# When ScalarE copies the transposed attention, and how many context steps stand ahead of the first norm's transposes in a decoder block

## The chip, the cores and the metric

One core of one Trainium2 chip. The metric is the device time of one launch in microseconds (us); lower is better. A run-time is given as the median of several runs.

## What is computed

A decoder block for 8 batch elements of 512 tokens, width 256, in float32. In words, for each batch element:

- `x = x + attn(layernorm(x))`: self-attention with 16 heads of 16, with learned relative-position terms on scores and values (clipped at a distance of 20), softmax, output projection `Wo`;
- `x = x + xattn(layernorm(x), ctx, ctx)`: a cross-attention without softmax over a context of 1601 rows of width 256, 16 heads of 64. Its inputs pass a layernorm with gain and bias; queries and keys are divided by their L2 norm per head. Behind it an MLP with GELU (width 1024), with residuals of its own;
- `x = x + ffn(layernorm(x))`: a gated feed-forward part (width 704) with blockwise 4-bit quantisation of inputs and weights.

Because the cross-attention has no softmax, `(qn kn^T) v` is computed as `qn (kn^T v)`: the context is folded once per batch element into a matrix per head, and then into one matrix `M` with the output projection.

## The kernel before

**Engines and order.** The kernel is written by engine: each of SyncE, GpSimd, ScalarE, VectorE and TensorE has a hand-written program, a loop over batch elements 0 to 6 (`batch(b, False)`) and a last round for element 7 (`batch(NB - 1, True)`). Each engine works strictly in its own written order; semaphores tie the orders together. The work is cut in T = 4 tiles of 128 tokens.

**The context steps.** While element b is in its tail (all that follows the attention's scores and softmax), the engines fold the context of element b + 1. This is cut in small steps, numbered s = -6 to 25, and each engine has a function `slot(nb, s)` with its share of step s. The 13 context tiles of 128 rows pass twice, each time for half of the heads, so that 26 steps accumulate. What an engine does in step s:

- TensorE (lines 1606 to 1635): two *ck matmuls* (keys of accumulation step s + 3; their moving operand is `cwk`, 512 wide), two *ct transposes* of context tile s + 4 (while there is such a tile), and for s >= 0 four *cg matmuls* which accumulate key-times-context in PSUM banks 4 and 5. At s = 0 and s = 13 the two banks are first zeroed with matmuls of `zeros`, at 13 after the first half has been read out (`evac_g`, L1264 on VectorE, L977 on ScalarE).
- ScalarE (lines 979 to 998): copy of the keys out of PSUM (L985), copy of the transposed context (L990), the squares of the keys (L995).
- VectorE (lines 1266 to 1308): statistics of context tile s + 6 (L1273 to L1278), sums of squares per head for step s + 2 (L1285, L1287), the norm's affine part for tile s + 5 (L1295, L1299), and the scaling of the keys of step s + 1 (L1306). Tiles end at 12, so the statistics end with s = 6 and the affine part with s = 7.
- GpSimd (lines 732 to 739): the inverse roots for both (L429, on `crs` and `crn`).

The waits are such that TensorE's step s needs VectorE's step s - 1 whole: the ct transposes wait for `caff_ready` (L1299), the cg matmuls for `cs_ready` (L1306):

```python
pe.wait_ge(caff_ready, ctile(nb, i))     # i = s + 4, made by VectorE's step s - 1
...
pe.wait_ge(cs_ready, cstep(nb, s))       # made by VectorE's step s - 1
```

VectorE's step s needs ScalarE's squares and GpSimd's roots of step s - 1 (the roots of the statistics too).

**Where the steps stand.** The table `SLOTS_AT` (line 79) puts the steps at named places of the tail, the same on the four engines, and each engine runs `slots(at)` where that place comes in its own order:

- `("band", t)`, steps -6 to -3: behind `weigh_band(t)` on TensorE, `combine(t)` on VectorE, and behind the copy L1136 on ScalarE;
- `("wo", t)`, steps -2 to 1: the output projection of the attention. TensorE (lines 1859 to 1880) transposes `Oraw` of tile t + 1, projects tile t (`project`, which waits for `aT_ready`; the row names `wo_s`), then does the step. ScalarE (lines 1138 to 1144) copies the transposed attention of tile t (L1142, which signals `aT_ready`), then does the step. VectorE (lines 1436 to 1442) adds the projection to `xin` (L1439), takes statistics (L1441), then does the step;
- `"ln"`, steps 2 to 5: TensorE does them directly behind the step of `("wo", 3)`, and only then transposes `Qn` (lines 1883 to 1887). VectorE first does the two chained norms (L1452 to L1467: aggregate, two inverse roots by GpSimd, `Qx`, `Qn`), then the steps, then half of `QnT` (L1471). ScalarE does the steps, then the other half of `QnT` (L1154). GpSimd does the steps between the norm's roots and the query norm's first root;
- `("x", -1)`, steps 6 to 8: behind the query projection of tile 0 (`project_q`, the row names `cwq`) on TensorE, behind the square L1151 on ScalarE, between the sum of squares L1476 of tile 0 and the scaling L1485 of tile 0 on VectorE, behind the query norm's root of tile 0 on GpSimd (L429 on `rn`);
- `("x", t)`, steps 9 to 18: within the cross-attention of tile t, behind the transposes of `qn`. TensorE waits for L1485 of tile t before it projects the queries of tile t + 1;
- `"yn"` and `("h", f)`, steps 19 to 25: norm and MLP.

The last round has no steps: in it `slots` does nothing.

Of the kernel before, what the change touches and what calls it, by code (L numbers as in the profile page):

```python
# [22 lines left out]
T = S // 128  # L23
# [53 lines left out]
LOADS = ((0, 1), (1, 4), (4, 8), (8, 12), (12, 13))  # L77
EQ = HG * 128
SLOTS_AT = {("band", 0): (-6,), ("band", 1): (-5,), ("band", 2): (-4,), ("band", 3): (-3,),
# [3 lines left out]
SLOTS_Q = (0, 0, 0, 1, 1, 1, 2, 2)  # L83
NORM_AT = 5
# [6 lines left out]
def build(nc, bass, mybir, d, out):  # L91
# [5 lines left out]
    with ctx:  # L97
# [147 lines left out]
        def bank(i, lo=0, hi=512, parts=128):  # L245
            return PS[0:parts, i * 512 + lo:i * 512 + hi]
# [726 lines left out]
        def _(act):  # L973
# [5 lines left out]
            def slot(nb, s):  # L979
                j = s + 3  # L980
                if 0 <= j < CSTEPS:
                    n = crows(j % CT)
                    act.wait_ge(ck_psum, cstep(nb, j))
                    act.wait_ge(cg_done, cstep(nb, j - 4))
                    act.activation(kns[0:n, j % 4, :], bank(6, parts=n), ACT.Copy).then_inc(kc_ready, 1)  # L985
                i = s + 4
                if 0 <= i < CT:
                    n = crows(i)
                    act.wait_ge(ct_psum, ctile(nb, i))
                    act.activation(cnT[:, i, :, 0:n], bank(7, 0, 256).rearrange("p (c t) -> p c t", c=2)[:, :, 0:n], ACT.Copy)\  # L990
                        .then_inc(ct_ready, 1)
                if 0 <= j < CSTEPS:
                    act.wait_ge(kc_ready, cstep(nb, j))
                    act.wait_ge(c_norm, cstep(nb, j - 2))
                    act.activation(csq[0:crows(j % CT), j % 2, :], kns[0:crows(j % CT), j % 4, :], ACT.Square)\  # L995
                        .then_inc(csq_ready, 1)
                if s == CT:
                    evac_g(nb, 0)
# [82 lines left out]
            def batch(b, final):  # L1081
                def slots(at):
                    for s in () if final else SLOTS_AT[at]:
                        slot(b + 1, s)
# [47 lines left out]
                for t in range(T):  # L1132
# [2 lines left out]
                        act.wait_ge(f_psum, T * b + t)  # L1135
                    act.activation(AT[:, t % 2, 0:4, :].rearrange("p a b -> p (a b)"), bank(0), ACT.Copy).then_inc(fa_act, 1)  # L1136
                    slots(("band", t))
                for t in range(T):
                    act.wait_ge(at_psum, T * b + t + 2)
                    if t >= 2:  # L1140
                        act.wait_ge(wo_psum, T * b + t)
                    act.activation(aT[:, t % 2, :, :].rearrange("p a b -> p (a b)"), bank(t % 2, 0, 256), ACT.Copy)\  # L1142
                        .then_inc(aT_ready, 1)
                    slots(("wo", t))
                slots("ln")

# [84 lines left out]
            with act.Fori(0, NB - 1) as b:  # L1231
                batch(b, False)
            batch(NB - 1, True)


# [865 lines left out]
```

## Time and profile before

| | |
|---|---|
| median of 3 runs | 2904.91 us (2897.34 to 2914.84) |
| the profiled execution | 2905.99 us, its span 2904.1 us |
| granted TensorE clock, mean | 0.955 |
| TensorE (matmul) busy | 2529.4 us, 87% |
| VectorE / GpSimd / ScalarE busy | 1705.5 / 1437.7 / 1180.0 us |
| chain that ended last | TensorE 64%, VectorE 9%, DMA 8%, issue 8%, ScalarE 6%, GpSimd 3% |

In the profile PE is the TensorE, PEld its weight loads, DVE the VectorE, ACT the ScalarE, POOL the GpSimd, SP the SyncE; L1142 is line 1142 of the kernel. L1601 is the helper through which all matmuls pass and L1604 that of all transposes, so matmuls are told apart by their operands. A float32 matmul shows as two records. In a timeline equal instructions are merged in one row; what follows in brackets is how long the engine was idle before the row and what ended this. A matmul's end overlaps the start of the next. PEclk is the granted TensorE clock as a share of full speed, 2.4 GHz; at 0.5 it is 1.2 GHz.

### The profile page before, as it was taken

The page shows a single profiled execution, that of the slowest core. Times are in us where ns is not written, and L with a number is a line of the kernel's source. Part 1 is how long each engine was busy: PE and PEld are TensorE (multiplying, and loading weights), DVE is VectorE, ACT ScalarE, POOL GpSimd, SP SyncE. Part 2 cuts the span into 40 slices and gives each one's busy share as a digit, 9 for nine tenths or more (in the row PEclk, how much of TensorE's full clock was granted, in tenths as well). Part 3 has the DMA queues.
Part 4 walks back from the last instruction along what each step waited for, and adds up shares of the span by engine and source line. Part 5 has one row for each costly group of instructions (what it writes and reads, how often), then busy time and mean ns, then how long its engine had stood idle before and what let it go on. Part 6 is the DMA issues. An engine that isn't in the chain of part 4 may idle for free.

```text
span 2904.1 us, 49839 instructions
## 1 busy us (share of the span) xinstructions
PE 2529.4 (87%) x14884; PEld 1734.0 (60%) x14884; DVE 1705.5 (59%) x3890; ACT 1180.0 (41%) x2089; POOL 1437.7 (50%) x1489
## 2 busy tenths in 40 slices
PE   3697899888998889988999889988899888998877
PEld 1365566665665656656566655666566565666645
DVE  4746644676446764566646665367654676456625
ACT  1237423382234722355333642338323472235511
POOL 2447444573545645365553745457344564436422
PEclk8799999998999999999999999999999999999989
DMA  8607200670007600284004720057100760028300
GB/s 244 140 0 167 59 1 8 143 181 25 1 27 166 163 1 1 70 160 126 1 8 100 177 71 1 8 132 181 36 1 22 167 167 1 1 68 160 104 0 8
DMA packets 403729, 224.59 MB, mean 77 GB/s; under 512 B 209822, under 2 KB 399542, under 8 KB 400438
## 3 DMA queue, kind: packets, MB, share of 16 engines
q1 hardware_dynamic: 370406, 215.76, 30.6%
q10 hardware_dynamic: 33024, 5.24, 1.6%
q8 instruction: 139, 2.28, 0.3%
q14 instruction: 160, 1.31, 0.2%
HBM read 129.15 MB, written 91.80 MB: 76 GB/s over the span
## 4 chain that ended last, share of the span: by engine, by line
PE 64%; DVE 9%; DMA 8%; issue 8%; ACT 6%; POOL 3%; SPq 1%; ACTq 0%; DVEq 0%; POOLq 0%
PE PS L1601 58%; PE PS L1604 7%; DMA prob_scr<-arena 5%; DMA arena<-bias_scr 2%; ACT arena L1104 1%; ACT arena L1097 1%; DVE PS L1377 1%; DVE ss L1476 1%; DVE arena L1306 1%; POOL rstd L429 1%; SPq L587 1%; ACT arena L1151 1%; POOL arena L769 1%; DVE arena L1295 1%; DVE css L1285 0%
## 5 line engine op out<-in xcount | busy, mean ns | idle before, releaser
L1601 PE MATMUL PS<-arena 128*17 128x128 f32 (+7 forms) x6656 | 746.5, 310 | 84.4 <-ACT arena L1097 66.9
L1601 PEld LDWEIGHTS PS<-arena 128*17 128x17 f32 (+2 forms) x6656 | 498.7, 123 | 272.8 <-issue 125.8
L1604 PE MATMUL PS<-ident,arena 128*128 128x128 f32 (+1 forms) x3312 | 520.3, 285 | 101.1 <-DVE arena L1299 31.1
L1604 PEld LDWEIGHTS PS<-ident,arena 128*128 128x128 f32 (+1 forms) x3312 | 390.4, 145 | 274.0 <-issue 92.4
L429 POOL TENSOR_TENSOR crn<-crn,mhalf 128x8 f32<-128x8 f32 (+1 forms) x208 | 373.5, 1802 | 115.8 <-DVE crn L1287 114.3
L1377 DVE CUSTOM_DVE_ANT_0 PS<-PS,arena 128x512 f32<-128x512 f32 x512 | 343.0, 711 | 125.1 <-POOL arena L769 89.5
L1601 PE MATMUL PS<-cwk,arena 128*128 128x512 f32 (+1 forms) x832 | 406.9, 613 | 2.6 <-ACT arena L990 2.6
L1097 ACT ACTIVATE arena<-PS,nmax 128x512 f32<-128x512 f32 x512 | 344.8, 695 | 113.7 <-DMA prob_scr<-arena 59.5
L985 ACT ACTIVATE arena<-PS 128x512 f32<-128x512 f32 (+1 forms) x208 | 124.2, 597 | 553.7 <-PE PS L1601 553.7
L769 POOL TENSOR_TENSOR arena<-arena 128x128 f32<-128x128 f32 x512 | 218.0, 459 | 102.7 <-DMA arena<-bias_scr 97.4
L1104 ACT ACTIVATE arena<-PS 128x512 f32<-128x512 f32 x384 | 232.5, 606 | 10.5 <-PE PS L1601 9.4
L429 POOL TENSOR_TENSOR rn<-rn,mhalf 128x16 f32<-128x16 f32 x32 | 93.0, 2906 | 286.9 <-DVE rn L1478 286.9
L1601 PEld LDWEIGHTS PS<-cwk,arena 128*128 128x128 f32 (+1 forms) x832 | 158.1, 194 | 126.9 <-issue 114.2
L429 POOL TENSOR_TENSOR crs<-crs,mhalf 128x1 f32<-128x1 f32 (+1 forms) x104 | 64.0, 615 | 271.4 <-DVE crs L1278 271.4
L1285 DVE TENSOR_REDUCE css<-arena 128x8 f32<-128x512 f32 (+1 forms) x208 | 141.7, 681 | 85.8 <-ACT arena L995 85.6
L1306 DVE TENSOR_TENSOR arena<-arena,crn 128x512 f32<-128x512 f32 (+1 forms) x208 | 142.6, 685 | 60.1 <-POOL crn L429 58.0
L870 POOL TENSOR_TENSOR arena<-arena,mass_mask 128x512 f32<-128x512 f32 x128 | 163.7, 1279 | 19.6 <-ACT arena L1097 19.5
L429 POOL TENSOR_TENSOR rstd<-rstd,mhalf 128x4 f32<-128x4 f32 (+1 forms) x48 | 44.7, 931 | 253.8 <-DVE rstd L442 170.3
L757 POOL TENSOR_TENSOR arena<-edge_mask,arena 128x512 f32<-128x512 f32 x128 | 134.4, 1050 | 28.5 <-POOL arena L769 20.3
L1601 PE MATMUL PS<-cwq,arena 128*128 128x512 f32 x256 | 120.6, 615 | 14.2 <-DVE arena L1471 7.2
L995 ACT ACTIVATE arena<-arena 128x512 f32<-128x512 f32 (+1 forms) x208 | 131.1, 630 | 3.6
L1601 PE MATMUL PS<-wdT,arena 128*128 128x256 f32 (+1 forms) x384 | 99.3, 401 | 32.3 <-ACT arena L1194 31.1
(162 smaller groups left out, 3654.9 us busy)
## 6 DMA issues: line engine op xcount, KB each, us to landing
arena<-bias_scr SPq DMA_DIRECT2D x128, 336.0 KB, 3.6
prob_scr<-arena SPq DMA_DIRECT2D x128, 336.0 KB, 4.6
q_scr<-arena SPq DMA_DIRECT2D x128, 128.0 KB
arena<-q_scr SPq DMA_DIRECT2D x128, 128.0 KB, 4.4
arena<-k_scr SPq DMA_DIRECT2D x16, 768.0 KB, 11.9
arena<-prob_scr SPq DMA_DIRECT2D x128, 80.0 KB, 3.4
arena<-far_scr SPq DMA_DIRECT2D x16, 546.0 KB, 7.8
arena<-in_ctx SPq DMA_DIRECT2D x16, 512.0 KB, 5.0
```

Source lines behind the costliest of these rows:

```text
L429: pool.tensor_tensor(x, x, mhalf[0:x.shape[0], 0:x.shape[1]], ALU.pow).then_inc(done, 1)
L757: pool.tensor_tensor(Eb, edge_mask[:].unsqueeze(1).broadcast_to([128, HG, 128]), bcast(Rb[:, t, g * HG:(g + 1) * HG, BAND], 128), ALU.mult ...
L769: pool.tensor_tensor(edge, edge, Eb[:, j, :], ALU.add).then_inc(far_added, 1)
L870: pool.tensor_tensor(prod[:], P[:, (g % 2) * HG:(g % 2 + 1) * HG, t * 128 + BAND:t * 128 + BAND + 128], mass_mask[:].unsqueeze(1).broadcas ...
L995: act.activation(csq[0:crows(j % CT), j % 2, :], kns[0:crows(j % CT), j % 4, :], ACT.Square)\
L1097: act.activation(P[:, (g % 2) * HG + j, PAD:PAD + S], bank(j), ACT.Exp, bias=nmax[:, j:j + 1], scale=-1.0).then_inc(probs_ready, 1)
L1104: act.activation(PTs[:, pt_slot(t, h), :], bank(t_bank(t, h)), ACT.Copy).then_inc(pt_copied[0], 1)
L1285: st(dve.tensor_reduce(css[0:n, j % 2, :], csq[0:n, j % 2, :].rearrange("p (h c) -> p h c", c=XD), AX.X, ALU.add))
L1306: dve.tensor_tensor(k, k, bcast(crn[0:n, j % 2, :], XD), ALU.mult).then_inc(cs_ready, 1)
L1377: dve.tensor_tensor_reduce(out=bank(j), in0=bank(j), in1=Wz[:, at:at + S], scale=-0.25, scalar=BIG, op0=ALU.add, op1=ALU.min, accum_out=nm ...
L1601: return pe.matmul(o, l, r, start=start, stop=stop, **kw)
L1604: return pe.transpose(o, i, ident[0:i.shape[0], 0:i.shape[0]])
```

## The change

The table moves steps: `"ln"` keeps only step 2; steps 3 to 6 stand at `("x", -1)`, 7 to 9 at `("x", 0)`, 10 to 12 at `("x", 1)`, 13 to 15 at `("x", 2)`, 16 to 18 at `("x", 3)`. All four engines with steps read this table. On ScalarE the copy of the transposed attention becomes a function; the copy of tile 0 comes first, and the copy of tile t + 1 comes ahead of the step of `("wo", t)`. The waits of the copy are what they were.

```diff
-            ("wo", 0): (-2,), ("wo", 1): (-1,), ("wo", 2): (0,), ("wo", 3): (1,), "ln": (2, 3, 4, 5),
-            ("x", -1): (6, 7, 8), ("x", 0): (9, 10, 11), ("x", 1): (12, 13, 14), ("x", 2): (15, 16), ("x", 3): (17, 18),
+            ("wo", 0): (-2,), ("wo", 1): (-1,), ("wo", 2): (0,), ("wo", 3): (1,), "ln": (2,),
+            ("x", -1): (3, 4, 5, 6), ("x", 0): (7, 8, 9), ("x", 1): (10, 11, 12), ("x", 2): (13, 14, 15), ("x", 3): (16, 17, 18),
             "yn": (19, 20, 21), ("h", 1): (22,), ("h", 3): (23,), ("h", 5): (24,), ("h", 7): (25,)}
...
-                for t in range(T):
+                def copy_attended(t):
                     act.wait_ge(at_psum, T * b + t + 2)
                     if t >= 2:
                         act.wait_ge(wo_psum, T * b + t)
                     act.activation(aT[:, t % 2, :, :].rearrange("p a b -> p (a b)"), bank(t % 2, 0, 256), ACT.Copy)\
                         .then_inc(aT_ready, 1)
+
+                copy_attended(0)
+                for t in range(T):
+                    if t + 1 < T:
+                        copy_attended(t + 1)
                     slots(("wo", t))
                 slots("ln")
```

## Rows read from the trace of the kernel before

**Rows 1.** The page: TensorE's busy time; the group of GpSimd's roots on `crn`.
```profile
PE 2529.4 (87%) x14884; PEld 1734.0 (60%) x14884; DVE 1705.5 (59%) x3890; ACT 1180.0 (41%) x2089; POOL 1437.7 (50%) x1489
...
L429 POOL TENSOR_TENSOR crn<-crn,mhalf 128x8 f32<-128x8 f32 (+1 forms) x208 | 373.5, 1802 | 115.8 <-DVE crn L1287 114.3
```

**Rows 2.** Whom TensorE waited for: us in total, times, longest us.
```profile
PE PS L1604 <- DVE arena L1299: 31.1, 8, 7.2
...
PE PS L1601 <- ACT arena L1142: 25.8, 22, 1.4
PE PS L1601 <- DVE arena L1264: 18.6, 7, 2.7
```

**Rows 3.** Timeline of TensorE, first batch's tail: start us, length us, instruction.
```profile
336.36 1.13 PE L1601 MATMUL PS<-wo_s,arena 128*128 128x256 f32 x4 [1.39 <-ACT arena L1142]
...
340.96 1.13 PE L1601 MATMUL PS<-wo_s,arena 128*128 128x256 f32 x4 [1.32 <-ACT arena L1142]
...
350.55 1.88 PE L1601 MATMUL PS<-cwk,arena 128*128 128x512 f32 x4
352.27 0.38 PE L1604 MATMUL PS<-ident,arena 128*128 128x128 f32 x2
...
354.21 1.88 PE L1601 MATMUL PS<-cwk,arena 128*128 128x512 f32 x4
359.29 0.44 PE L1604 MATMUL PS<-ident,arena 128*128 128x128 f32 x2 [3.20 <-DVE arena L1299]
...
370.60 1.04 PE L1604 MATMUL PS<-ident,arena 128*128 128x128 f32 x8
372.55 3.70 PE L1601 MATMUL PS<-cwq,arena 128*128 128x512 f32 x8 [0.91 <-DVE arena L1471]
...
387.61 3.70 PE L1601 MATMUL PS<-cwq,arena 128*128 128x512 f32 x8
```

**Rows 4.** Timeline of ScalarE, same tail: the copy of tile 1.
```profile
335.92 0.39 ACT L1142 ACTIVATE arena<-PS 128x256 f32<-128x256 f32 x1
```

**Rows 5.** Timeline of VectorE, same tail: output projection, norm, steps 2 and 3.
```profile
337.53 0.42 DVE L1439 TENSOR_TENSOR xin<-xin,PS 128x256 f32<-128x256 f32 x1 [1.07 <-PE PS L1601]
...
341.05 0.69 DVE L1306 TENSOR_TENSOR arena<-arena,crn 128x512 f32<-128x512 f32 x1
...
351.21 0.37 DVE L1452 BATCH_NORM_AGGREGATE mv<-bnst 128x2 f32<-128x6 f32 x4
...
355.14 1.38 DVE L1467 TENSOR_SCALAR arena<-xin,mv,rstd 128x256 f32<-128x256 f32 x4
356.44 0.42 DVE L1273 BATCH_NORM_STATS2 cbn<-arena 128x6 f32<-128x256 f32 x1
...
359.76 0.42 DVE L1273 BATCH_NORM_STATS2 cbn<-arena 128x6 f32<-128x256 f32 x1
```

**Rows 6.** Timeline of VectorE and GpSimd, same tail, beside the first query norm.
```profile
377.34 1.22 DVE L1476 TENSOR_REDUCE ss<-arena 128x16 f32<-128x1024 f32 x1 [4.85 <-ACT arena L1151]
...
380.36 0.48 DVE L1295 SCALAR_TENSOR_TENSOR arena<-arena,cmv,rows 128x256 f32<-128x256 f32 x1
...
386.35 1.22 DVE L1485 TENSOR_TENSOR arena<-PS,rn 128x1024 f32<-128x1024 f32 x1
...
378.95 2.90 POOL L429 TENSOR_TENSOR rn<-rn,mhalf 128x16 f32<-128x16 f32 x1 [8.87 <-DVE rn L1478]
```

**Rows 7.** Stretches of TensorE: from:to, length, busy (instructions), granted clock, DMA share, GB/s.
```profile
350.50:372.50 22.00, 17.78 (x65) 0.92 0.00 1
695.50:719.70 24.20, 19.86 (x71) 0.86 0.00 1
...
2082.60:2103.40 20.80, 16.29 (x67) 1.00 0.00 1
...
361.00:363.40 2.40, 2.40 (x8) 0.57 0.00 0
...
418.10:420.00 1.90, 1.90 (x5) 0.50 0.00 0
```

## The prediction

> **What bounds the kernel now.** I read the page first: TensorE is busy 87% of the span [rows 1], so only its idle time and its clock can be won; time saved elsewhere counts where it shortens a wait of TensorE. Next the list of what TensorE waited for [rows 2]. Two entries touch the change: 25.8 us in 22 waits for ScalarE's copies of the transposed attention (L1142), and 31.1 us in 8 waits for VectorE's affine step L1299. The longest of these, 7.2 us, is in the start-up; the other seven are one per batch, 3.4 us each. Then the timeline of one batch tail, the first, for TensorE [rows 3], ScalarE [rows 4] and VectorE [rows 5, 6], and at last the granted clock of the stretch between the output projection and the query projection, which is below full speed in six of the seven looped batches [rows 7].
>
> The reader should see two things in rows 3. The projections of tiles 1 and 2 wait for L1142 (1.39 and 1.32 us). After the ck matmuls of context step 3, started at 354.21, TensorE idles 3.20 us until VectorE, which came late out of the norm (L1452 to L1467), has done L1299 of step 2. So TensorE is bound here by VectorE's order of work.
>
> **Part one: the copy one tile ahead.** Nothing is added or removed; copies of 0.39 us change places with context steps on ScalarE [rows 4]. Tile 0's copy still stands behind the step of ("band", 3), so its wait stays: 25.8 less seven times 2.71 is 6.8 us in the 8 batches. Tile 3's copy was in time already. Tiles 1 and 2 lose their waits: 1.39 + 1.32 = 2.7 us, and with the 0.16 us of matmul tail that a wait exposes each time (ck matmuls 1.88 long, the next started 1.72 after them), 3.0 us of TensorE. The new copy of tile t+1 needs the transposes of t+1 and the projection of t-1, both issued before TensorE's step, and nothing is queued behind it that is due earlier: TensorE ends step 2 at 351.2 instead of 354.2. In the final batch there are no steps, so the order is as before and worth nothing. No DMA is in any moved step, so SyncE's queue is unchanged.
>
> VectorE gains less. Per tile it needs 0.80 us for L1439 and L1441 and 3.4 us for its step, 4.2 us from 337.53 to the end of L1306 at 341.73 [rows 5], while TensorE now needs 3.66 for the step (350.55 to 354.21), 1.13 - 0.16 = 0.97 for the projection and some 0.2 for two of the transposes, 4.8 us. Starting tile 1 at 336.4, when its step -2 is done, in place of 337.53, it runs back to back and reaches the norm at 348.95 in place of 351.21: 2.3 us earlier.
>
> **Part two: one step ahead of the transposes.** The last Qn tile is ready 5.31 us after L1452 starts (351.21 to 356.52), now at 354.3, the first at 353.3. TensorE is through with step 2 at 351.37: it idles 1.95 us, then transposes along, to 354.65. VectorE, by its own order, does step 2 before it turns to QnT: step 2 takes 3.32 us (the pitch 356.44 to 359.76), then L1471 0.81 us [rows 5]; the query projection can start at 358.3. So a second wait of 3.65 us stands there, in place of 0.91. What the removal of three steps frees on TensorE is only cover. Idle before, per batch: 3.4 + 0.16 + 0.9 = 4.5 us; after: 1.95 + 3.65 = 5.6.
>
> **Part three: four steps beside the first query norm.** Steps 3 to 6 now stand between query projection 0 and query projection 1. VectorE enters them 2.6 us after TensorE's projection ended: ScalarE's square, then the sum L1476 (377.34 and 1.22 long, its small follower 0.1; T0 is 372.55 + 3.70 - 0.17 = 376.1) [rows 6]. All four steps are full ones, with statistics and the affine part: 4 x 3.32 = 13.3 us, then the scaling L1485, 1.2 us: 17.1 us after T0. TensorE's own four steps take 4 x 3.66 + 0.16 = 14.8. Before, the three steps there, two of them shorter on VectorE, ended level with TensorE (L1485 from 386.35 to 387.57, projection 1 at 387.61 without a wait [rows 3, 6]). So a wait of 2.2 us is new. GpSimd: root of the query norm 2.90 us, then 2.4 us per step (1.8 for L429 on crn [rows 1], some 0.6 on crs); the scale of step 3's group is there 8.2 us after T0, needed at 8.6, and each later one earlier than VectorE needs it. GpSimd hides behind VectorE, by 0.4 us at the tightest. On ScalarE the steps pass the QnT copy and the square, both ready to run; it is idle between.
>
> Later groups: three steps each. VectorE's steps from 8 on have no norm: a sum and L1306, 0.7 us each, and small ones, 1.6 us against TensorE's 3.66 - 0.22 = 3.44, so x1 to x3 keep TensorE busy. The wait before the zeroing matmuls of step 13 (L1264, 2.66 us [rows 2]) changes its place, not its size: VectorE must now do the sum, 1.22, a copy of a bank, some 0.7, and its step 13 first, which again ends 2.7 us after the ck matmuls.
>
> **The clock.** After the 3.20 us wait the row from 361.00 shows 0.57 granted, 1.2 GHz most of the time; the level before was 2.4 GHz [rows 7]. Over the stretch between the projections the loss (one minus the grant, times the length) is 1.76 us in the batch shown; four more are like it (0.92 of 22.2 to 22.4 us), one lost 3.39 (0.86 of 24.2), one nothing (1.00). Together 12.3 us, 1.76 per batch. After the change the norm has 5.6 us of idle with 1 us of transposes between; bounds are 0 (the one batch at 1.00) and 3.4 (the worst). I take 1.7, the common value, since it is again one spell of waiting. For the new 2.2 us wait the nearest is that of 2.66 us before step 13, after which 1.90 us ran at 0.50 and more at a part. Bounds 0 (no dip) and 1.7 (the common loss); I take 1.0, nearer to the latter, since the wait is nearly as long.
>
> **The sum, per looped batch.** Before: 1.39 + 1.32 + 3.4 + 0.16 + 0.9 + 1.76 = 8.9 us. After: 1.95 + 3.65 + 2.2 + 1.7 + 1.0 - 0.17 (one exposed tail fewer) = 10.3. Difference +1.4, times 7 is +10 us. Against this execution's own 2905.99 us that gives 2916; the median of the runs is 1.1 us lower, hence **2915**, +0.35%. About 0.5%, 14.5 us, is what a measurement of this kernel can tell from no change.
>
> **A rule against the change.** Through a root of GpSimd (378.95, 2.90 us) VectorE ran L1295, an operation with two SBUF inputs, from 380.36 in its usual 0.48 us [rows 6]. The Trainium skill, SBUF — State Buffer, section "Who interferes with whom", says that a VectorE instruction with two SBUF inputs contends with a GpSimd instruction that reads SBUF, and that the loser blocks fully. By that rule L1295 would have waited to 381.85; the trace disagrees.
>
> **Rivals.**
> *Clock rival, slower:* its place is the two waits just named. If the engine restarts each time at 1.2 GHz for the long spell of the second batch (3.4 lost) and loses 1.7 after the 2.2 us wait, the sum is 7.6 + 5.1 - 8.9 = +3.8 per batch, +27 us: 2932. It decides, that is passes 0.5%, once the losses exceed 3.4 us per batch (idle alone differs by +0.45). For it: the waits come closer together and are longer than today's. Against: a dip inside steps 3 to 6 is hidden by the 2.2 us wait.
> *No dips, a little faster:* idle alone after, 7.6, against 8.9: -1.3, -9 us: 2896. For it: one batch in seven stayed at 1.00. Against: six did not.
> *Faster:* VectorE does not end last beside the query norm, and there is no dip: 5.6 - 0.1 - 8.9 = -3.4, -24 us: 2881. It needs VectorE's four steps to take under 11 us in place of 13.3; the pitch of 3.32 us, its instructions back to back, speaks against that.
> *Port rival, slower:* VectorE's two-input work of a step (two of 0.48 and L1306's 0.69, 1.65) and GpSimd's 2.35 take turns, 4.0 us a step: 4 x 0.7 + 1.5 = 4.3 more per batch, +30 on 2915: 2945. The row above speaks against it. This is the rule that the Trainium skill's SBUF — State Buffer states.
> *The change does not do what it says:* this is true in part and in my sum, for tile 0 and the final batch.
>
> **How the numbers follow.** Forecast 0.42; no dips 0.18; faster 0.10; clock rival 0.27; port rival 0.03. The range runs from 2891, just under the no-dip case less a few us for the run-to-run spread, to 2934, just above the clock rival; it leaves out the faster and the port case and a few per cent of spread. The forecast's own range is 2905 to 2923. Faster by over 0.5% (under 2890.4) is the faster rival and a little of the no-dip case, 0.12. Slower (over 2919.4) is the clock rival nearly whole, the port rival and a little of the forecast, 0.31. The rest, 0.57, is the same.
>
> **What would show each step.** L1142 waits fall from 22 to 8 (one per batch), some 7 us. L1299 loses the seven waits of 3.4 us; in their place stand seven of about 2 us for L1467 and seven of 3.6 us for L1471 in place of 0.9, and seven of 2.2 us for L1485. L1264 stays at seven of 2.7. The granted clock between the projections says which of the clock cases holds. I am wrong if TensorE shows no wait ahead of query projection 1, or if the L1142 waits of tiles 1 and 2 stay.

## The result, and the profile after

The changed kernel took 2922.9 us (median of 8 runs) against 2903.5 us for the kernel before, timed beside it: a ratio of **1.0053, 95% interval [1.0033, 1.0073]**, some 15 us (10 to 21) slower. The forecast was 2915 us, +10 us; the result is inside the range and on the edge between "the same" and "slower by over 0.5%". The profiled execution has a span of 2924.3 us, 20.2 more than before.

The page, TensorE's line and the roots on `crn` (they answer to [rows 1]):

```profile
PE 2547.8 (87%) x14884; PEld 1738.0 (59%) x14884; DVE 1704.5 (58%) x3890; ACT 1179.7 (40%) x2089; POOL 1438.0 (49%) x1489
...
L429 POOL TENSOR_TENSOR crn<-crn,mhalf 128x8 f32<-128x8 f32 (+1 forms) x208 | 374.8, 1806 | 163.7 <-DVE crn L1292 162.2
```

TensorE has the same 14884 matmuls and is busy 18.4 us longer with them: most of what this profile lost is not waiting but the same matmuls running slower. Not all of it belongs to the change. TensorE's busy time inside the stretches of lower granted clock, halved, gives what the lower clock cost. Between the first output projection and query projection 2 of the seven looped batches this went from 11.4 to 19.9 us, 8.5 more. The other 10 us of the 18.4 lie mostly in the start-up and the last round, which hold no moved step: the start-up alone lost between 15 and 24 us in the twelve profiles of this study. Whom TensorE waited for (us in total, times, longest); the change shifts the lines behind it by 5: L1304 is what was L1299, L1472 L1467, L1476 L1471, L1490 L1485, L1269 L1264 [rows 2]:

```profile
PE PS L1606 <- DVE arena L1476: 25.9, 8, 3.7
PE PS L1606 <- DVE arena L1490: 21.6, 8, 6.9
PE PS L1609 <- DVE arena L1472: 20.9, 8, 5.5
PE PS L1606 <- DVE arena L1269: 18.6, 7, 2.7
...
PE PS L1609 <- DVE arena L1304: 7.2, 2, 6.9
...
PE PS L1606 <- ACT arena L1142: 6.3, 7, 1.2
```

The waits for ScalarE's copy fell by 19.5 us and those for the affine step by 23.9; in their place came 15.4 for Qn, 18.7 for QnT and 14.7 for the scaled queries (against 5.5, 7.2 and 6.9 us before, the first and the last of these in the final batch alone). The five come to +5.4 us: waiting was traded for waiting. The timeline of TensorE in the first tail and, in its last three rows, in the second and third shows where, and what followed [rows 3]:

```profile
336.37 1.03 PE L1606 MATMUL PS<-wo_s,arena 128*128 128x256 f32 x4
...
348.95 1.88 PE L1606 MATMUL PS<-cwk,arena 128*128 128x512 f32 x4
...
354.68 1.41 PE L1609 MATMUL PS<-ident,arena 128*128 128x128 f32 x8 [1.90 <-DVE arena L1472]
359.69 5.38 PE L1606 MATMUL PS<-cwq,arena 128*128 128x512 f32 x8 [3.60 <-DVE arena L1476]
...
382.41 3.70 PE L1606 MATMUL PS<-cwq,arena 128*128 128x512 f32 x8 [1.77 <-DVE arena L1490]
...
703.32 5.94 PE L1606 MATMUL PS<-cwq,arena 128*128 128x512 f32 x8 [3.73 <-DVE arena L1476]
...
726.74 3.70 PE L1606 MATMUL PS<-cwq,arena 128*128 128x512 f32 x8 [2.15 <-DVE arena L1490]
...
1050.58 6.38 PE L1606 MATMUL PS<-cwq,arena 128*128 128x512 f32 x8 [3.27 <-DVE arena L1476]
```

The projection of tile 1 (336.37) waits for nothing now. The transposes wait 1.90 us, the query projection 3.60, and that projection then takes 5.38 us for the matmuls that took 3.70 [rows 3]. It is so in all seven looped batches: 5.38, 5.94, 6.38, 6.20, 5.23, 5.95 and 5.31, 40.4 us against 25.9, so 14.5 us lost to a slow clock. Query projection 1, behind the third wait, took 5.40 instead of 3.70 in two batches: 3.4 us. The granted clock over query projection 0 in the second and third batch:

```profile
703.32:709.10 5.78, 5.78 (x9) 0.61 0.01 3
1050.58:1056.80 6.22, 6.22 (x8) 0.56 0.01 3
```

That is the level of 1.2 GHz for most of the stretch, against 1.00, 2.4 GHz, over the same projection before. In five batches this spell of 1.2 GHz begins during the wait for QnT and lasts 6.8 us; in the other two it begins within 0.4 us of the end of the wait for Qn and lasts 10.2 us. Before there was one of 3.4 us in five batches, one of 6.8 us in the second and none in the sixth. TensorE is busy for less than the whole spell, because a part of it lies over the wait (first and fourth batch):

```profile
356.30:363.13 6.83, 3.44 (x4) 0.50 0.00 0
1393.90:1404.14 10.24, 7.00 (x14) 0.50 0.00 1
```

VectorE in the first tail, the counterpart of [rows 5] and [rows 6]:

```profile
350.29 0.38 DVE L1457 BATCH_NORM_AGGREGATE mv<-bnst 128x2 f32<-128x6 f32 x4
...
354.21 1.38 DVE L1472 TENSOR_SCALAR arena<-xin,mv,rstd 128x256 f32<-128x256 f32 x4
355.51 0.42 DVE L1278 BATCH_NORM_STATS2 cbn<-arena 128x6 f32<-128x256 f32 x1
...
358.83 0.81 DVE L1476 TENSOR_SCALAR arena<-PS,cols 128x512 f32<-128x512 f32 x1
...
367.50 0.42 DVE L1278 BATCH_NORM_STATS2 cbn<-arena 128x6 f32<-128x256 f32 x1
...
381.14 1.22 DVE L1490 TENSOR_TENSOR arena<-PS,rn 128x1024 f32<-128x1024 f32 x1
```

VectorE is through with Qn at 355.6, works 3.3 us on step 2, and makes its half of QnT only at 358.83, although the transposes that it needs ended at 356.1. Beside the query norm it enters the steps at 367.50 and scales the queries from 381.14, 13.6 us later, which is four steps (3.68 us for the first, 3.3 for the others).

### The profile page after: what moved, and what is told of

It is laid out like the page before. It is cut to its first block, busy times and chain, and to the rows that moved or that the text cites. A ratio compares the mean times of both kernels' runs of the same rounds, so it can differ in the third digit from the quotient of the medians.

```text
span 2924.3 us, 49839 instructions
## 1 busy us (share of the span) xinstructions
PE 2547.8 (87%) x14884; PEld 1738.0 (59%) x14884; DVE 1704.5 (58%) x3890; ACT 1179.7 (40%) x2089; POOL 1438.0 (49%) x1489
## 4 chain that ended last, share of the span: by engine, by line
PE 60%; DVE 12%; DMA 8%; issue 8%; ACT 5%; POOL 3%; SPq 3%; DVEq 0%; ACTq 0%; POOLq 0%
PE PS L1606 54%; DMA prob_scr<-arena 6%; PE PS L1609 6%; DMA arena<-bias_scr 2%; DVE arena L1311 1%; ACT arena L1104 1%; POOL crs L429 1%; DVE arena L1300 1%; SPq L587 1%; ACT arena L1097 1%; DVE cbn L1278 1%; DVE PS L1382 1%; DVE ss L1481 1%; POOL rstd L429 1%; ACT arena L1156 1%
## 5 line engine op out<-in xcount | busy, mean ns | idle before, releaser
L1606 PE MATMUL PS<-arena 128*17 128x128 f32 (+7 forms) x6656 | 738.0, 308 | 80.5 <-ACT arena L1097 65.2
L1606 PEld LDWEIGHTS PS<-arena 128*17 128x17 f32 (+2 forms) x6656 | 492.4, 122 | 265.4 <-issue 117.2
L429 POOL TENSOR_TENSOR rn<-rn,mhalf 128x16 f32<-128x16 f32 x32 | 93.0, 2905 | 279.1 <-DVE rn L1483 279.1
L1606 PE MATMUL PS<-cwq,arena 128*128 128x512 f32 x256 | 140.5, 700 | 47.5 <-DVE arena L1476 25.9
L1311 DVE TENSOR_TENSOR arena<-arena,crn 128x512 f32<-128x512 f32 (+1 forms) x208 | 142.6, 686 | 47.0 <-POOL crn L429 45.5
L1156 ACT ACTIVATE arena<-PS 128x1024 f32<-128x1024 f32 x32 | 32.8, 1024 | 248.1 <-PE PS L1606 248.1
```

The lines of the kernel that those rows point to most:

```text
L429: pool.tensor_tensor(x, x, mhalf[0:x.shape[0], 0:x.shape[1]], ALU.pow).then_inc(done, 1)
L1311: dve.tensor_tensor(k, k, bcast(crn[0:n, j % 2, :], XD), ALU.mult).then_inc(cs_ready, 1)
L1606: return pe.matmul(o, l, r, start=start, stop=stop, **kw)
```

## The experiments

All ratios are against the kernel before on the same chip. Where two kernels are compared, their ratios are divided and taken of 2905 us. The ten experiments ran in three groups (copy alone, table alone, three steps, QnT first; then zeros, six steps and the two mends together; then zeros in the old table and step 13), the changed kernel in a fourth. Across groups both intervals count, so that a difference against the changed kernel is known to about 8 us either way.

**The two edits apart.** One kernel has the copy one tile ahead and the old table, the other the new table and the old copies:

```diff
 # copy alone, against the changed kernel: SLOTS_AT as before
-            ... ("wo", 3): (1,), "ln": (2,),
-            ("x", -1): (3, 4, 5, 6), ("x", 0): (7, 8, 9), ...
+            ... ("wo", 3): (1,), "ln": (2, 3, 4, 5),
+            ("x", -1): (6, 7, 8), ("x", 0): (9, 10, 11), ...
...
 # table alone, against the kernel before: the new SLOTS_AT
-            ... ("wo", 3): (1,), "ln": (2, 3, 4, 5),
-            ("x", -1): (6, 7, 8), ("x", 0): (9, 10, 11), ...
+            ... ("wo", 3): (1,), "ln": (2,),
+            ("x", -1): (3, 4, 5, 6), ("x", 0): (7, 8, 9), ...
```

> The copy one tile ahead, with the table of before. My theory: the L1142 waits of tiles 1 and 2 go (2.7 us of the 3.7 per batch), VectorE reaches the norm 2.3 us earlier, and since TensorE's step 3 still waits for VectorE (L1299), VectorE's 2.3 us is the gain: 7 x 2.3 = 16 us faster, ratio 0.9945; the wait for L1299 grows from 3.4 to some 4 us per batch. Rival one: the copy gives its whole 3.0 us, 21 us faster, ratio 0.993. Rival two: the copy gives nothing, since VectorE's chain was last anyway: ratio 1.000, and the L1299 wait grows by the full 3 us.

> The new table of steps, with the copies of before. My theory: the table is what loses. With the copy worth -16 us and both together +15 us, the table alone is +31 us, ratio 1.011; the waits for the QnT half (3.6 us) and the scaled queries (about 2.2 us) stand there as in the changed kernel. Rival: the two edits need each other (the copy worth nothing or a loss alone): then this is +15 us or less, ratio 1.005.

The copy alone: **0.9955 [0.9934, 0.9976]**, 13 us faster. The table alone: **1.009 [1.0058, 1.0121]**, 26 us slower. The two add up to +13 us, against +15 (10 to 21) measured for both together. The rival with no gain from the copy falls, and so does the one in which the edits need each other; the rival with the copy's whole 3.0 us (0.993) lies just outside the interval. In the copy's profile the wait for the affine step has grown, from 31.1 to 37.3 us, 0.9 per batch, because VectorE won less than TensorE:

```profile
PE PS L1609 <- DVE arena L1304: 37.3, 8, 7.2
```

**Three steps beside the query norm instead of four.**

```diff
-            ("x", -1): (3, 4, 5, 6), ("x", 0): (7, 8, 9), ...
+            ("x", -1): (3, 4, 5), ("x", 0): (6, 7, 8, 9), ...
```

> The changed kernel with three context steps (3 to 5) beside the first query norm and four (6 to 9) in the next group. My theory: the wait for the scaled queries of tile 0 is VectorE's fourth step of 3.3 us, so it vanishes, the time per looped batch falls by 2.2 us of waiting and up to 1.7 us of slow clock after it: 15 to 27 us faster than the changed kernel, ratio to before 0.996 to 1.000. Rival: the loss is only in the wait ahead of the query projection, and the work is merely moved: as the changed kernel, ratio 1.005, with the wait of 2 us standing before the projection of tile 2 instead.

**1.0062 [1.004, 1.0085]**, no gain. My expectation was wrong. The rival's time, 1.005, is within the interval, but its mechanism is not what happened, since the wait did not move to tile 2 either. It stands where it stood (timeline of TensorE, then of VectorE, first tail):

```profile
378.82 3.70 PE L1606 MATMUL PS<-cwq,arena 128*128 128x512 f32 x8 [2.12 <-DVE arena L1490]
```

```profile
367.23 0.42 DVE L1278 BATCH_NORM_STATS2 cbn<-arena 128x6 f32<-128x256 f32 x1
...
377.55 1.22 DVE L1490 TENSOR_TENSOR arena<-PS,rn 128x1024 f32<-128x1024 f32 x1
```

The arithmetic was at hand: with n full steps VectorE needs 2.6 + 3.32 n + 1.2 and TensorE 3.66 n, so a full step less makes VectorE's lag longer by 0.3, not shorter by 3.3. Measured are 0.2: the wait is 2.37 us in six batches where it was 2.15. The total of all waits for L1490 went from 21.6 to 23.3 us. Before the change three steps hid the chain, by this reckoning because two of them (7 and 8) are cheaper on VectorE. The next run tests that.

**Six steps beside the query norm.** If the lag is VectorE's 3.8 us of query work, cheap steps behind the full ones pay it back:

```diff
-            ("x", -1): (3, 4, 5, 6), ("x", 0): (7, 8, 9), ("x", 1): (10, 11, 12), ("x", 2): (13, 14, 15), ("x", 3): (16, 17, 18),
+            ("x", -1): (3, 4, 5, 6, 7, 8), ("x", 0): (9, 10, 11), ("x", 1): (12, 13, 14), ("x", 2): (15, 16), ("x", 3): (17, 18),
```

> The changed kernel with six context steps (3 to 8) beside the first query norm, and 9 to 18 placed as in the kernel before. After the run with three steps my theory is: what counts there is how much VectorE's steps cost against TensorE's. VectorE spends a fixed 3.8 us on sum and scaling, a heavy step (up to 6) costs it 3.3 us against TensorE's 3.66, a light one (8) 1.6 against 3.44. With three or four heavy steps VectorE ends 2.2 to 2.5 us late; with 3 to 8 VectorE needs 2.6 + 4 x 3.3 + 2.8 + 1.6 + 1.2 = 21.4 us and TensorE 21.8, so the wait for the scaled queries is gone in the looped batches and with it the slow clock after it: 15 to 27 us faster than the changed kernel, ratio to before 0.996 to 1.000. Rival: VectorE or GpSimd is late by a fixed amount however many steps stand there (GpSimd's roots 2.9 + 6 x 2.4 = 17.3 us start 2.7 us late and end the group): the wait of 2 us stays and the ratio is 1.005.

**0.9993 [0.9975, 1.0011]**, 17 us under the changed kernel. The seven waits of 2.1 us that went make 15 of them, and query projection 1 takes 3.60 us in all looped batches where two had lost 3.4 together. VectorE scales at 383.57 and TensorE gets there at 386.12 without waiting (timelines of VectorE and TensorE, first tail):

```profile
383.57 1.22 DVE L1490 TENSOR_TENSOR arena<-PS,rn 128x1024 f32<-128x1024 f32 x1
```

```profile
386.12 3.60 PE L1606 MATMUL PS<-cwq,arena 128*128 128x512 f32 x8
```

L1490 is waited for once, 6.9 us in the final batch. So neither VectorE nor GpSimd is late there by a fixed amount, and the rival falls. Query projection 0 is as slow as in the changed kernel (14.1 us lost in the seven batches): its waits were not touched.

**QnT ahead of step 2 on VectorE.**

```diff
-                slots("ln")
                 dve.wait_ge(qnT_psum, b + 2)
                 dve.tensor_scalar(QnT[:, 1, :], bank(1), ...).then_inc(qnT_ready, 1)
+                slots("ln")
```

> The changed kernel, but VectorE makes its half of QnT (L1476) ahead of context step 2 instead of behind it. My theory: the 3.6 us wait ahead of the query projection falls to 0.9 us (transposes to QnT), step 2 on VectorE hides behind that projection (3.5 us), so 2.7 us of waiting per looped batch go, plus up to 1.7 us of slow clock: 19 to 31 us faster than the changed kernel, ratio to before 0.995 to 0.998. Rival: the next step is then late on VectorE and the time comes back as a wait for its affine part (L1304) or its scaling (L1311) in step 3: ratio 1.004 or more.

**0.9964 [0.9943, 0.9986]**, 26 us under the changed kernel. The wait ahead of query projection 0 is 0.91 us in every batch, and nothing is late behind it but what was. The clock hardly came back: that projection takes 3.70 us in the first and third batch, but 5.40 to 6.64 in the other five (timeline of TensorE, first and second tail; the line of QnT is L1475 here):

```profile
356.10 3.70 PE L1606 MATMUL PS<-cwq,arena 128*128 128x512 f32 x8 [0.91 <-DVE arena L1475]
...
365.44 0.44 PE L1609 MATMUL PS<-ident,arena 128*128 128x128 f32 x2 [0.26 <-DVE arena L1304]
...
377.14 3.70 PE L1606 MATMUL PS<-cwq,arena 128*128 128x512 f32 x8 [1.78 <-DVE arena L1490]
...
699.59 6.37 PE L1606 MATMUL PS<-cwq,arena 128*128 128x512 f32 x8 [0.90 <-DVE arena L1475]
```

The 2.7 us of waiting explain 19 of the 26 us. The lower clock cost 17.0 us from the output projection to query projection 2 where it had cost 19.9, so it explains 3; the last 4 are within what two runs in different groups can tell. In the kernel before a wait of 0.9 us stood ahead of this projection too, without the wait of 2.2 us for Qn ahead of the transposes, and the projection took 3.70 us each time. So the wait for Qn seems enough for a slow spell here; no run removed it by itself.

**The clock by itself.** The waits stay as long as they are, but TensorE fills them with matmuls of zeros whose result nobody reads:

```diff
+                def fill(k, n):
+                    for _ in range(0 if final else n):
+                        mm(bank(k), zeros[:], zero_row, True, True, skip_group_check=True)
+
+                fill(2, 6)      # ahead of the wait for Qn
...
+                fill(2, 10)     # ahead of the wait for QnT
...
+                fill(0, 5)      # ahead of the wait for the scaled queries
```

> The changed kernel with matmuls of zeros (bf16, 512 wide, results unused) put in TensorE's three new waits: 6 ahead of the wait for Qn, 10 ahead of the wait for QnT, 5 ahead of the wait for the scaled queries. The waits end when they ended before, so the zeros cost nothing as long as they fit (0.21 us each at full clock). My theory: half of the change's loss is clock that falls because TensorE stands idle; with the waits filled the granted clock between the projections stays near 1.00 and 12 to 20 us come back: ratio to before 0.998 to 1.001. Rival: the clock's falls do not come from these waits, or zeros do not hold it: the time stays at ratio 1.005 or more, and the granted clock in the stretch from query projection 0 to 1 stays near 0.91.

**0.9993 [0.9974, 1.0011]**: 17 us came back for 147 more instructions. The table, the copies and every other engine's program are those of the changed kernel. TensorE's timeline in the first tail, and the stretches from the first projection of the output to query projection 0 and on to 1. The waits are not filled to their ends:

```profile
352.49 2.32 PE L1606 MATMUL PS<-zeros 128*128 128x512 bf16 x10
356.26 3.70 PE L1606 MATMUL PS<-cwq,arena 128*128 128x512 f32 x8 [1.45 <-DVE arena L1476]
...
375.37 1.24 PE L1606 MATMUL PS<-zeros 128*128 128x512 bf16 x5
377.30 3.70 PE L1606 MATMUL PS<-cwq,arena 128*128 128x512 f32 x8 [0.69 <-DVE arena L1490]
```

```profile
329.81:356.26 26.45, 24.39 (x100) 1.00 0.00 1
356.26:377.30 21.04, 19.93 (x70) 1.00 0.00 0
```

In the changed kernel the same two stretches are:

```profile
333.25:359.69 26.44, 20.93 (x85) 0.94 0.00 0
359.69:382.41 22.72, 20.52 (x64) 0.92 0.00 1
```

Both query projections take 3.70 us in all seven looped batches. The slow matmuls of the two in the changed kernel were 14.5 + 3.4 = 17.9 us, and 17 came back (9 to 25 with both intervals). That idle time lowers the clock here is thus shown by a run; what it costs agrees with what the trace had lost. Expected were 12 to 20 us and a clock near 1.00, and so it came.

**Zeros in the old table.** The copy alone, with 12 such matmuls in the wait for L1304 in step 3:

```diff
+                    if s == 3 and fill is not None:
+                        fill()          # 12 matmuls of zeros into bank 0
                     pe.wait_ge(caff_ready, ctile(nb, i))
```

> The copy one tile ahead, the table of before, and 12 matmuls of zeros on TensorE in the wait ahead of step 3's ct transposes (4 us there in the run with the copy alone). It tells how the two tables stand once the clock is held in both. My theory: the slow clock between the projections (16.9 us by length in that run, some of it in idle time) goes, 8 to 14 us below the copy alone, ratio to before 0.991 to 0.993; so the new table is worse by its waits too, about 7 us per mill of nothing more than the 1 us per batch of extra idle time (ratio 0.999 with zeros). Rival: the old table gains nothing from zeros, ratio 0.9955: then the clock's loss was the new table's alone.

**0.9918 [0.9902, 0.9935]**, 11 us under the copy alone, as expected. The old table lost to the clock as well: in the traces the lower clock cost 14.1 us between the output projection and query projection 0 in the copy alone and 3.4 with the zeros, 10.7 less. With the waits filled in both, the new table is still 0.75% (22 us) behind the old one: so the clock is not the whole of the table's cost. The waits come near to the rest: without zeros they are, per batch, 2.2, 3.6 and 2.1 us (7.9) in the changed kernel, where the copy alone waits (37.3 - 7.2)/7 = 4.3 for the affine step and 0.9 for QnT (5.2). The difference is 7 x 2.7 = 19 us of the 22, which are known to 7 us either way.

**The mends together.** Six steps and QnT first, then the same with zeros (6 ahead of Qn, 2 ahead of QnT):

> Both mends: six steps beside the first query norm, and VectorE's half of QnT ahead of step 2. Waits of TensorE between the output projection and query projection 1 per looped batch: 1.9 (Qn) + 0.9 (QnT), against 7.2 before. My theory: 20 us below the run with QnT first alone, ratio to before 0.987 to 0.991. Rival: the gains overlap (VectorE is late once, wherever): ratio 0.994 to 0.996.

> As the run with both mends, with 6 matmuls of zeros ahead of the wait for Qn and 2 ahead of the wait for QnT. If idle TensorE is what lowers the clock, the slow spells that are left after these two waits go too: up to 1.7 us per batch, 0 to 12 us below the run with both mends. If not: the same time or slightly slower.

**0.9894 [0.9854, 0.9933]** and **0.9848 [0.982, 0.9876]**. The gains of the two mends add up (17 and 26 us under the changed kernel apart, 46 together), so the rival in which they overlap, 0.994 to 0.996, falls. The last has the lowest median of the study, 2864.8 us against 2912.4 for the kernel before on that chip; it beats both kernels. The difference made by the zeros is 13 us, a little over the 0 to 12 expected, with intervals that overlap, so the timing alone does not prove it. The traces bear it out: without zeros query projection 0 takes 3.70 us in the first batch and 5.40 to 6.68 in the other six, 14.3 us lost, and with them 3.70 in all seven. The third tail, first without, then with zeros:

```profile
1045.17 6.43 PE L1606 MATMUL PS<-cwq,arena 128*128 128x512 f32 x8 [0.91 <-DVE arena L1475]
```

```profile
1031.55 3.70 PE L1606 MATMUL PS<-cwq,arena 128*128 128x512 f32 x8 [0.47 <-DVE arena L1475]
```

**Step 13's wait filled too.** Nine more matmuls of zeros there:

```diff
+                        if s and fill is not None:
+                            fill()      # waits for qt_act, qt_dve of tile 1; 9 matmuls into bank 0
                         if s:
                             pe.wait_ge(g_act, PASSES * nb + 2)
```

> The best version so far (six steps, QnT first, zeros ahead of Qn and QnT) with 9 more matmuls of zeros in the wait of 2.7 us of step 13. If idle time lowers the clock there too, the stretch from query projection 2 to 3 goes to a granted clock of 1.00 in every batch (it lost 4.8 us in the profile of that version, 8 us in others): 5 to 10 us less, ratio 0.981 to 0.983. Rival: those falls have another cause, or the zeros delay the read-out of the banks: the same or slower than 0.985.

**0.9845 [0.9825, 0.9864]**: not to be told from 0.9848. The clock did what was expected: from query projection 2 to 3 it is at 1.00 in all seven batches, and the seven stretches together are 149.4 us against 154.5. Those 5 us are 0.2%, which the timing cannot resolve. Inconclusive as to time.

## Why the forecast was right, and where it was off

- **The copy.** Forecast 3.0 us of TensorE, 2.3 us of VectorE per batch. The copy alone gave 13 us (7 x 2.3 is 16), within its interval of 7 to 19. The tile 0 wait stayed, 6.3 us in 7 waits where 6.8 in 8 were expected.
- **One step ahead of the transposes.** Forecast waits of 1.95 and 3.65 us; measured in the looped batches (20.9 - 5.5)/7 = 2.2 and (25.9 - 0.9)/7 = 3.6. The step order on VectorE is the cause of the second; the run with QnT first cuts it to the 0.9 us of before.
- **Four steps beside the query norm.** Forecast 2.2 us, measured (21.6 - 6.9)/7 = 2.1. The size was right. But I had put it as if the number of steps made it; the runs with three and with six show that it is their kind: full steps hardly pay back VectorE's 3.8 us, cheap ones do.
- **Step 13** kept its seven waits of 2.7 us at another place, as forecast, and a slow spell behind five of them, as before.
- **The clock.** Here the number was right by luck. Forecast after the change were 2.7 us per batch, taken by the length of the slow spells. By that measure it was 4.4 us: the spells were two to three times as long as the common one of before. But 22 of their 61 us lay over idle time, where they cost nothing, so that the matmuls lost 19.9/7 = 2.8 us (14.5/7 = 2.1 in query projection 0, 3.4/7 = 0.5 in query projection 1, the rest in the transposes). The split was off as well: 1.7 and 1.0 were forecast behind the two waits.
- **The sum.** The waits grew by 0.8 us per batch, as the terms of the forecast say, 5.4 us in all. The lower clock cost 8.5 us more, where the forecast had 2.7 - 1.76 = 0.9 per batch, 6.6. Part of that is the term before: I took 1.76 us of slow clock by length. TensorE was busy 17.8 to 17.9 us in the stretches at 0.92 and 16.29 in the one at 1.00 [rows 7], so the matmuls lost 1.5 to 1.6 us there, and 11.4/7 = 1.6 over all seven. Waits and clock come to 14 us, or 12 with the exposed tails and the small wait of 0.16 us counted as in the forecast. The timing gives +15 (10 to 21), the forecast was +10. The profiles' own difference, 20 us, has some 10 us in places that the change leaves alone, so this pair of executions cannot be used to fit the sum any closer.
- **The rivals.** The clock rival, +27 us, was right in its condition and wrong in its price: a spell of 6.8 us or more, the long spell of the second batch, came in all seven looped batches. It cost 2.1 us in query projection 0 and not 3.4, because a part of it lay over the wait; and behind the third wait a spell came in two batches of seven only. The no-dip case did not occur. The port rival falls: VectorE's four steps took 3.3 to 3.5 us each beside GpSimd's roots, once 3.7. By my estimate from the rule of the Trainium skill (SBUF — State Buffer, "Who interferes with whom") they would have taken 4.0; the trace does not agree on that side.

## What to carry to other kernels

When work is moved as cover from one wait to another, cost it on every engine that shares it, against the engine that should be covered: here a full step covers 3.66 us of TensorE but occupies VectorE, the engine being waited for, for 3.32. And look at what the late engine does just before the operation that is waited for: moving one statement of VectorE ahead of a step won back 26 us, as much as the whole table lost. A wait costs more than its length where the next matmuls run at the lower clock; cheap matmuls without use in an unavoidable wait won that back in three kernels here. Price a slow clock by the busy time in it: its length overstates it where it lies over a wait.

## What the runs showed of the hardware

Matmuls of zeros (bf16, 0.21 us each) kept the granted clock at 1.00 from the output projection to query projection 1 in all seven looped batches, although their operands are all zeros and the wait for QnT was not filled to the end (1.45 to 1.57 us were left). Of the waits of 2.7 us ahead of step 13, five of seven had a slow spell behind them before and after the change; of those of 2.1 us for the scaled queries, two of seven.

GpSimd's small root on `crs` took 0.54 to 0.56 us in 67 of its 104 executions in the changed kernel, and 0.63 to 1.04 us in the other 37. All 37 began while VectorE was in an operation with two inputs in SBUF (L1300 or L1311), and the more of this was left the longer they took: 0.63 us with 0.22 left, 0.77 with 0.36, 0.81 with 0.39, 1.04 with 0.62. The root at 373.26 began with 0.09 us of L1300 left and took 0.55, although L1304, another such operation, began within it (timelines of VectorE and GpSimd, changed kernel):

```profile
370.58 0.68 DVE L1311 TENSOR_TENSOR arena<-arena,crn 128x512 f32<-128x512 f32 x1
...
372.87 0.48 DVE L1300 SCALAR_TENSOR_TENSOR arena<-arena,cmv,rows 128x256 f32<-128x256 f32 x1
373.50 0.48 DVE L1304 SCALAR_TENSOR_TENSOR arena<-arena,crs,rows 128x256 f32<-128x256 f32 x1
```

```profile
370.64 1.04 POOL L429 TENSOR_TENSOR crs<-crs,mhalf 128x1 f32<-128x1 f32 x1
...
373.26 0.55 POOL L429 TENSOR_TENSOR crs<-crs,mhalf 128x1 f32<-128x1 f32 x1
```

So here a GpSimd root that begins during such an operation of VectorE seems to wait for its end. The other way round nothing is seen: 28 executions of L1300 or L1304 and 15 of L1311 lay wholly within GpSimd's roots of 2.90 us on `rn` and took their usual 0.48 and 0.68 us. No run was made to separate this from other causes, and the profile's durations on GpSimd are rough.
